# A head's output in cross attention made whole in the next head's first step, in place of two halves in two steps

## The reference

```
x = x + attention(layernorm(x))                     # 16 heads, biases, Wq Wk Wv Wo
x = x + gamma * cross(layernorm(x), ctx, ctx)       # q, k, v as (batch, rows=channels, 512)
x = x + ffn(layernorm(x))                           # ternary w1, w3, w2: silu(h1) * h3, then w2

def cross(q, k, v):                                 # 8 heads of 64 rows each
    qk  = einsum('bhdq,bhdl->bhql', qh, kh) / 8     # 512 x 512 per head
    sm  = softmax(qk)                               # over l
    ret = einsum('bhql,bhdl->bhdq', sm, vh)         # 64 x 512 per head
```

## Time and profile before

| | |
|---|---|
| median of three runs | 1171.01 us (1170.23 to 1171.52) |
| the profiled execution | 1170.35 us |
| its span, first to last instruction | 1168.6 us |
| PE busy | 1118.9 us, 96% |
| PEld busy | 938.8 us, 80% |
| DVE busy | 743.5 us, 64% |
| ACT busy | 551.6 us, 47% |
| POOL busy | 461.0 us, 39% |

### The profile page before, as it was taken

The page is one execution under the profiler, slowest core; times in us unless marked ns, Lnnn a source line. Parts: engine busy times, 40 slices in busy tenths (PEclk is TensorE's granted clock), DMA queues, the critical chain, the costliest instruction groups (busy, mean ns, idle before and its releaser), DMA issues.

```text
span 1168.6 us, 15784 instructions
## 1 busy us (share of the span) xinstructions
PE 1118.9 (96%) x5792; PEld 938.8 (80%) x5792; DVE 743.5 (64%) x1389; ACT 551.6 (47%) x1145; POOL 461.0 (39%) x400
## 2 busy tenths in 40 slices
PE   4999999989999999999999999989999999999997
PEld 4888888868888788888888888768878887887776
DVE  7555547887757677765423325878767876787431
ACT  2455673324242366577514223267628753774230
POOL 1322327331432265664334030157517642764030
PEclk9999999999999999999999999999999999999999
DMA  7466654434433634312521022271113111310000
GB/s 234 132 181 180 197 162 138 163 112 146 143 115 121 204 91 120 98 37 98 225 72 55 18 97 82 94 201 47 46 56 107 46 47 64 99 46 11 27 1 36
DMA packets 53846, 121.13 MB, mean 104 GB/s; under 512 B 10009, under 2 KB 10009, under 8 KB 51722
## 3 DMA queue, kind: packets, MB, share of 16 engines
q1 hardware_dynamic: 53770, 120.13, 32.6%
HBM read 102.27 MB, written 17.84 MB: 103 GB/s over the span
## 4 chain that ended last, share of the span: by engine, by line
PE 83%; DVE 7%; ACT 4%; issue 2%; POOL 2%; DMA 1%; SPq 0%; POOLq 0%; DVEq 0%; ACTq 0%
PE bank L150 17%; PE bank L151 17%; PE bank L152 17%; PE bank L538 6%; PE bank L539 6%; PE bank L501 4%; PE bank L552 4%; PE bank L553 4%; PE bank L523 2%; PE bank L524 2%; PE bank L511 2%; PE bank L512 2%; POOL wal L1917 1%; DMA kd<-in_ctx 1%; ACT wah L1378 1%
## 5 line engine op out<-in xcount | busy, mean ns | idle before, releaser
L538 PE MATMUL bank<-x3h,w 128*128 128x512 f32 (+1 forms) x352 | 141.8, 403 | 2.4 <-DVE x3l L795 1.7
L1356 ACT ACTIVATE yh<-bank 128x512 fp32r<-128x512 f32 x64 | 38.1, 600 | 214.2 <-PE bank L152 214.1
L539 PE MATMUL bank<-x3l,w 128*128 128x512 f32 (+1 forms) x352 | 138.9, 394 | 0.0
L875 POOL TENSOR_SCALAR pe_x<-pe_x,xri,gam 128x512 f32<-128x512 f32 x96 | 75.6, 788 | 79.7 <-DVE xri L726 75.6
L150 PE MATMUL bank<-yh,rh 128*128 128x512 f32 x256 | 101.1, 395 | 6.0 <-DVE xacc L1779 6.0
L150 PE MATMUL bank<-wah,gh 128*128 128x512 f32 x256 | 103.9, 406 | 2.6 <-POOL wal L1917 1.3
L1917 POOL TENSOR_TENSOR wal<-raw_a,wah 128x512 fp32r<-128x512 f32 x44 | 59.7, 1382 | 117.2 <-ACT wah L1378 117.2
L722 DVE TENSOR_REDUCE xmx<-bank 128x1 f32<-128x512 f32 x128 | 87.5, 683 | 24.1 <-PE bank L512 23.3
L1922 POOL TENSOR_TENSOR wbl<-raw_b,wbh 128x512 fp32r<-128x512 f32 x64 | 88.6, 1408 | 36.0 <-ACT wbh L1398 35.8
L1615 DVE TENSOR_TENSOR yl<-bank,yh 128x512 fp32r<-128x512 f32 x64 | 44.0, 690 | 90.8 <-ACT yh L1356 90.6
L150 PE MATMUL bank<-wah,ph 128*128 128x512 f32 x256 | 100.4, 392 | 0.3 <-POOL wal L1917 0.3
(11 more groups left out here) (171 smaller groups left out, 3026.5 us busy)
## 6 DMA issues: line engine op xcount, KB each, us to landing
raw_a<-in_wk SPq DMA_DIRECT2D x8, 1024.0 KB, 5.3
raw_b<-in_wq SPq DMA_DIRECT2D x8, 1024.0 KB, 5.3
raw_a<-in_wo SPq DMA_DIRECT2D x8, 1024.0 KB, 5.1
raw_b<-in_wvt SPq DMA_DIRECT2D x8, 1024.0 KB, 4.9
ternary_scratch<-wraw SPq DMA_DIRECT2D x24, 341.2 KB, 2.9
x1d<-x_scratch SPq DMA_DIRECT2D x48, 128.0 KB, 3.1
kd<-in_ctx SPq DMA_DIRECT2D x48, 128.0 KB, 3.1
w<-ternary_scratch SPq DMA_DIRECT2D x2, 2730.0 KB, 10.8
```

The costliest lines, as they stand in the source:

```text
L538: pe.matmul(u_bank[w][0:m, :], lhs, x3h[:, c, :], start=c == 0, stop=False)
L539: mm = pe.matmul(u_bank[w][0:m, :], lhs, x3l[:, c, :], start=False, stop=c == CK - 1)
L875: pool.tensor_scalar(m.pe_x[:, q, :], m.pe_x[:, q, :], xri[:, q:q + 1], gam[:], ALU.mult, ALU.mult).then_inc(s["xpn"], 1)
```

## The change

`pe_ret` stays for batch 0. The turns use a new function that does all 512 columns of a head at once, after waiting for the fourth quarter's `pxl`, and both increments of `r_ready` come from its last matmul:

```
+        def pe_ret_whole(pe, b, h):
+            n = b * XH + h
+            pe.wait_ge(s["t_free"], t_p(b, h, 3) + 1)
+            pe_wait(pe, "r_free", n, 1)
+            for c in range(CK):
+                lhs = main.vts[:, h % 4, c, :]
+                pe.matmul(main.r[:], lhs, main.pxh[:, c, :], start=c == 0, stop=False)
+                mm = pe.matmul(main.r[:], lhs, main.pxl[:, c, :], start=False, stop=c == CK - 1)
+            mm.then_inc(s["r_ready"], 2)
...
                         if q == 0 and h % 2 == 0:
                             pe_vt(pe, main, b, h)
+                        if q == 0 and h >= 2:
+                            pe_ret_whole(pe, b, h - 2)
                         if h:
                             pe_pt(pe, main, b, h - 1, q)
-                        if q == 1 and h >= 2:
-                            pe_ret(pe, main, b, h - 2, 1)
-                        if q == 3 and h >= 1:
-                            pe_ret(pe, main, b, h - 1, 0)
...
             if b is not None:
+                pe_ret_whole(pe, b, XH - 2)
                 pe_pt(pe, main, b, XH - 1, 0)
-                pe_ret(pe, main, b, XH - 2, 1)
...
                 pe_pt(pe, main, b, XH - 1, 3)
-                pe_ret(pe, main, b, XH - 1, 0)
-                pe_ret(pe, main, b, XH - 1, 1)
+                pe_ret_whole(pe, b, XH - 1)
```

## The result

The changed kernel takes 1189.26 us (median; 1188.95 to 1191.61) against 1170.62 for the one before: 1.0164 times as long, 95% interval 1.0147 to 1.0182, +18.6 us. A second measurement beside the experiments gave 1.0174 (1.0157 to 1.0191). The profiled execution took 1191.61 us, its span is 1189.8. First line: the page's busy times, which answer to the earlier trace rows.

A forecast was written before the change was run, and what follows sets the result against it. PE, busy 96%, was the bound, with DVE close behind. Turns 2, 3 and 1 added 4.6 + 4.6 + 5.7 = 14.9 us to 1170.35, giving 1185.3; with 0.66 for the median 1185.9, said as 1186, range 1175 to 1191.

The forecast's parts named there:

- The loop: PE and DVE, once per head: ret waits for px(h-2,3) and delays px(h-1,0); adds 0.64, 0.31, 2.43, nothing, 1.65 us.
- The matmuls: A head's ret as 8 matmuls of 512 columns, not 16 of 256: -0.7 us in three turns, 0 to -1.4.
- D: Distance on DVE from px(h,3) to px(h+1,0), 4.00 us where ret had to wait.
- The wait for vts: First step of head 4: ret(2) covers the wait before pt(3,1), worth up to 0.85 us a turn.
- S: Time from px(h,0) to px(h,3); before the change 7.20, 8.38, 7.71, 7.96, 8.20 us for h = 1 to 5.
- before head 3's quarters: Place in turn 2 where the distance D, 3.36 us before, was to grow by 0.64.
- Rivals 1, 2 and 4: Whole kernel: loop doesn't close, 1177.6 (0.14); ret never late, 1167.7 (0.06); fixed part per matmul saved, 1176 with loop (0.02).
- rival 3: Also late: q and k before sx(h+1,0), or exp freeing score banks; +20 to +25 us, 1193; chance 0.08.
- S is DVE's queue itself: From px(h,0) to px(h,3), claimed that DVE's own queue sets the time; 7.20 to 8.38 us before.
- The lag before the end of the turn: Turn 2: px(6,0) 4.85 us later, PE's real lag about 4.0, less 0.3 for small DVE idles swallowed.
- The end of the turn: ret(7) has no cover: pt(7,3) to down 1 grows from 3.08 to 4.00 us, +0.9 a turn.
- The clock: PE's granted clock, 1.00 in the windows read: waits of 1 to 2 us no longer than now, no change.

The follow-up runs named there:

- e1: Changed kernel with the size undone: ret whole at the new place with its one wait, but as sixteen matmuls of 256 columns; 1192.49 us, 1.0192.
- e3: Kernel before, with only the first half of ret(h-2) moved to step (h,0) ahead of pt(h-1,0); 1167.36 us, 0.9974.
- e2: Kernel before, with only the second half of ret(h-2) moved to step (h,0) ahead of pt(h-1,0); 1175.65 us, 1.0048.
- e7: Changed kernel with second copies of pxh and pxl for odd heads and ret whole behind pt(h-1,1) in step (h,1); 1172.42 us, 1.0014.
- e6: Changed kernel with the up piece of step 18 put into step 19, on all engines; 1187.25 us, 1.0140.
- e11: Changed kernel with DVE's q and ACT's two preparations ahead of px(h-1,0), in odd heads alone; 1189.48 us, 1.0160.
- e5: Changed kernel with DVE's q and moments ahead of px(h-1,0) in a head's first step; 1188.36 us, 1.0156.
- e4: Changed kernel with ret(7), at the end of a turn, in two halves of 256 again; 1188.52 us, 1.0150.
- e9: Changed kernel with turn 1 in the old order, the two halves at their old places; 1185.05 us, 1.0122.

## Why the prediction was right, and where its size was off

The time, 1189.26, lies in the range (1175 to 1191) at its upper end; the forecast said +14.9 and it was +18.6. The loop that gives it is shown by the runs; the 3.7 us that it is short have two causes, below.

- **The matmuls**, -0.7: right in kind, too small in size. e1 puts the wide form at -0.6 a turn, -1.8 in all, beyond the bound of -1.4: the wide ones stand 0.231 us apart and not 0.235. D has it in its 3.95.
- **The wait for vts** goes: right, pt(3,1) starts without one. It was 0.75 us in distances of starts (914.11 - 912.45 in the earlier trace rows, less 0.44 and 0.47), not 0.85; the sum doesn't use it, the first two rivals do. e3 shows what that is worth where nothing comes for it.
- **The loop**: right, to the hundredth in places. D forecast 4.00, measured 3.95 (4.21 at ret(2)), and at ret(4) too, where PE was to stay the bound at 4.38; S for heads 1 to 3 forecast 7.7, 8.4, 7.7, measured 7.74, 8.39, 7.72. pt(4,0) forecast 4.03 late, measured 4.24. The 0.64 called "before head 3's quarters" stands before head 2's, px(2,0). ret(3) idles 1.63 us, ret(5) 0.84, ret(7) 1.41, where 1.5 to 2.5, about 1 and about 1.4 were given. e2, e3, e7 each switch it off or shorten it in their own way, and e6 and e11 take 0.7 and 1.2 out of S and find it again at the turn's end. Rivals 1, 2 and 4 fall: the loop closes, ret is late, and the wide matmuls save 1.8 and not 10 us. Of rival 3 little is there: one sx waits 0.38 us for an exp, once a turn, at a place that costs nothing (below).
- **S is DVE's queue itself**: wrong as worded. DVE had no idle there because it was just fed; e5 shows ACT's queue is only 0.2 us shorter. It did not change the sum, since both queues were in the distances read.
- **The lag before the end of the turn**: this term was too small. In turn 3 px(6,0) is 5.20 us later than before where 4.85 was said, of which 0.2 is ret(2): DVE, itself late, frees the bank for the up piece of step 15 late (0.87 us), a place that I had priced at nothing. The 0.38 us before sx(5,0) cost nothing, for ret(3) behind it waits 1.63 anyway. From 4.85 I took 0.85 as moved work and 0.3 for small idles that a late DVE swallows, which gives 3.7; px(7,0) is 4.64 later, for S of head 6 gets only 0.54 shorter (7.38 to 6.84). That is 0.9 too little, and turn 3 is +5.48 where +4.6 was said. Turn 2 is the same without its 1.6 of the clock, and turn 1 without its 2.1 is +6.7 where +5.7 was said. So it is 0.9 in each of the three turns, 2.7 of the 3.7 missing.
- **The end of the turn**, +0.9 for ret(7): e4 gives back 0.85.
- **The clock**: this step failed. I wrote that waits of 1 to 2 us are no longer than those now and took no change. In the first profiled execution ret(1) of turn 1 came behind 4.5 us of waiting and ran at half clock, and ret(3) of turn 2 likewise behind 1.6 us: 1.63 and 1.31 us in those blocks alone (3.58 and 3.26 against 1.95), 2.1 and 1.6 with what stands behind them. That execution has 3.7 us of it, the median about 1, by the estimate from executions of equal clock: the rest of the 3.7 missing. What decides in which execution the clock falls is open.

## What to carry to other kernels

A block that waits for the last result of another engine should not stand in front of the work which that engine needs next: ask of each wait not how long it is but what stands behind it, and sum the loop (the longer of the two queues, and the path from its last result back to its first). Splitting the block so that its ready half goes first and the waiting half behind the next producer was worth more than doing it in one piece; here the ready half in front was a gain (0.9974), the whole a loss (1.0164), and a second buffer, with which the whole one could stand behind the transposes again, made it nearly harmless (1.0014).

## What the runs showed of the hardware that was not expected

TensorE's granted clock can fall to half behind a wait of only 1.6 to 1.7 us, and need not: equal waits at ret(3) in turns 2 and 3 of one execution ended at 0.56 and 1.00, and the first up piece of the last turn ran at 1.00 before and at 0.54 in e9, behind the same 1.7 us; sx(3,1) of turn 1 went on at 1.00 before and at 0.50 in e9, behind the same 2.6 us. One fall lengthened a turn by 1.0 us (e9, turn 1), 1.6 (turn 2) and 2.1 (turn 1). So kernels with the same instructions in a stretch differ there by several us (the last turn, the same in all but e6, took 67.5 to 72.0), and a change of 1.2 us a turn (e11) can be plain in the trace of a turn and not be seen in a median of four or five runs. The mean granted clock of each execution helps: compare those where it is equal. Matmuls of 256 and 512 columns in this type cost 0.120 and 0.231 us from start to start, the same per column within 4%.
